# Expert weights that arrive transposed, a program per tile count, and a deferred last down block

## The reference, cut to what matters

```python
slot = jnp.where(kept, experts * C + pos, E * C)
buf = jnp.zeros((E * C + 1, D), x.dtype).at[slot].set(xf[tokens])
xb = buf[:E * C].reshape(E, C, D)
gu = jnp.einsum('ecd,efd->ecf', xb, w12)          # w12: (E, 4096, 512)
g, u = jnp.split(gu, 2, axis=-1)
h = jax.nn.silu(g) * u
yb = jnp.einsum('ecf,edf->ecd', h, w3).reshape(E * C, D)   # w3: (E, 512, 2048)
ys = yb[jnp.minimum(slot, E * C - 1)] * (weights * kept.astype(weights.dtype))[:, None]
out = jnp.zeros((T, D), x.dtype).at[tokens].add(ys)
```

## Time and profile before

| | us |
|---|---|
| median of 3 runs | 3138.96 (3138.65 to 3143.81) |
| profiled execution: span from first to last instruction | 3142.4 |
| first stage, up to the first weight load of the second | 599.4 |
| second stage | 2543.0 |
| TensorE (PE) busy | 3009.2 (96%) |
| VectorE (DVE) busy | 1519.7 (48%) |
| ScalarE (ACT) busy | 1078.7 (34%) |

### The profile page before, as it was taken

How to read it: one execution, slowest core, us unless ns; L and a number is a source line. 1 busy time by engine, 2 the same in 40 slices (tenths; PEclk the granted TensorE clock), 3 DMA queues, 4 the chain that set the end, 5 groups by cost and what they waited for, 6 DMA issues and landing times.

```text
span 3142.4 us, 58679 instructions
## 1 busy us (share of the span) xinstructions
PE 3009.2 (96%) x21454; PEld 2800.7 (89%) x21455; DVE 1519.7 (48%) x3173; ACT 1078.7 (34%) x2999; POOL 412.9 (13%) x393
## 2 busy tenths in 40 slices
PE   6999999599999999999999999999999999999998
PEld 5888888599998999989998999899998999899887
DVE  5777777344444444444444444444444444444444
ACT  5776765122223222232223322322223222332333
POOL 3545554100002000010001000200002000100110
PEclk9999999699999999999999999999999999999999
DMA  7421221311112210230113211220113211321321
GB/s 257 171 86 68 95 74 68 128 55 41 40 40 51 76 40 26 48 92 25 40 40 75 77 41 40 65 76 21 40 41 53 76 40 40 55 91 60 76 89 51
DMA packets 120226, 209.69 MB, mean 67 GB/s; under 512 B 11628, under 2 KB 45180, under 8 KB 119970
## 3 DMA queue, kind: packets, MB, share of 16 engines
q1 hardware_dynamic: 103330, 174.77, 15.8%
q0 software_dynamic: 16640, 31.69, 5.2%
HBM read 145.06 MB, written 67.70 MB: 68 GB/s over the span
## 4 chain that ended last, share of the span: by engine, by line
PE 78%; issue 2%; DVE 1%; ACT 0%; DMA 0%; ACTq 0%; POOL 0%; DVEq 0%; SPq 0%; POOLq 0%
PE bank L1367 71%; PE bank L1382 6%; DVE yacc L1325 0%; DVE w_lo L1288 0%; ACT w_hi L1222 0%; ACT slotsT_hi L1222 0%; DMA raw<-in_L_ffn_w_dram 0%; DVE slotsT_lo L1288 0%; ACT yout L1255 0%; POOL out_dram L1179 0%; DVEq L1058 0%; ACTq L1214 0%; ACTq L1058 0%; DVEq L1035 0%; DVE h_lo L1309 0%
## 5 line engine op out<-in xcount | busy, mean ns | idle before, releaser
L1367 PE MATMUL bank<-slotsT_hi,w_hi 128*128 128x256 f32 x4352 | 1242.2, 285 | 37.5 <-issue 37.5
L1367 PE MATMUL bank<-slotsT_lo,w_hi 128*128 128x256 f32 x4352 | 1223.8, 281 | 0.0
L1367 PE MATMUL bank<-slotsT_hi,w_lo 128*128 128x256 f32 x4352 | 1222.6, 281 | 0.0
L1367 PEld LDWEIGHTS bank<-slotsT_hi,w_hi 128*128 128x128 f32 x4352 | 825.5, 190 | 43.6 <-issue 39.5
L1367 PEld LDWEIGHTS bank<-slotsT_lo,w_hi 128*128 128x128 f32 x4352 | 825.1, 190 | 4.1
L1367 PEld LDWEIGHTS bank<-slotsT_hi,w_lo 128*128 128x128 f32 x4352 | 823.5, 189 | 0.0
L1305 DVE TENSOR_TENSOR h<-silu,bank 128x256 f32<-128x256 f32 x544 | 229.1, 421 | 835.9 <-PE bank L1367 835.9
L1241 ACT CAST h_hi<-h 128x256 fp32r<-128x256 f32 x544 | 221.1, 406 | 814.7 <-DVE h L1305 814.7
L1325 DVE TENSOR_TENSOR yacc<-bank,yacc 128x512 f32<-128x512 f32 x441 | 304.6, 691 | 226.3 <-PE bank L1367 216.1
L1367 PE MATMUL bank<-w_hi,h_hi 128*128 128x512 f32 x1008 | 399.2, 396 | 5.8 <-issue 4.3
L1179 POOL DMA_INDIRECT out_dram<-yout,token x63 | 98.1, 1557 | 2317.2 <-ACT yout L1255 2305.5
(11 more groups left out here) (157 smaller groups left out, 3071.1 us busy)
## 6 DMA issues: line engine op xcount, KB each, us to landing
raw<-in_L_ffn_w_dram SPq DMA_DIRECT2D x195, 512.0 KB, 4.4
xrow<-expert_rows SPq DMA_DIRECT2D x41, 520.0 KB, 8.9
expert_rows<-zeros SPq DMA_DIRECT2D x40, 520.0 KB, 7.6
xin<-in_x_dram SPq DMA_DIRECT2D x16, 512.0 KB, 3.5
xres<-in_x_dram SPq DMA_DIRECT2D x16, 512.0 KB, 3.5
out_dram<-xres SPq DMA_DIRECT2D x16, 512.0 KB, 3.5
probs<-in_L_xattn_Wq_dram SPq DMA_DIRECT2D x1, 1024.0 KB, 8.7
probs<-in_L_xattn_Wo_dram SPq DMA_DIRECT2D x1, 1024.0 KB, 6.2
```

The source lines that it names most:

```text
L1367: last = nc.tensor.matmul(out_ap, st, mv, start=(at == 0), stop=(at == n - 1))
```

## The change

The host lays both weight tensors out anew, as one array with the contraction on the partitions, each chunk's 1.5 MB contiguous by partition. The kernel loads a chunk with one DMA, and ACT and DVE split it straight from SBUF; PE transposes no weights. In place of the branches in each chunk, every engine picks once per expert among eight complete programs, one for each number of tiles from 3 to 10 (`by_tiles`). Each cuts its tiles into blocks of 2, 3 or 4 tiles (256, 384 or 512 slots), without a padded tile. The down products of a chunk's last block are made after the first gate and up block of the next chunk. In the last chunk the next expert's first four token tiles are transposed between the down products (`closing`).

```diff
-            def blocks(eng, n_e, g1, g2, skip, between, half, end):
+            BLOCKS = {3: (3,), 4: (2, 2), 5: (3, 2), 6: (3, 3), 7: (4, 3), 8: (4, 4), 9: (3, 3, 3), 10: (4, 3, 3)}
+            TILES = sorted(BLOCKS)
+            XA = 4
...
+            def units_at(nt, q):
+                plan = {1: ((0, 1), (2, 3)), 2: ((0,), (1, 2), (3, 4), (5,)), 3: ((0,), (1,), (2,), (3,), (4,), (5,))}
+                return plan[len(BLOCKS[nt])][q]
+            def late_units(nt):
+                return (4, 5) if len(BLOCKS[nt]) == 1 else ()
...
+            def by_tiles(eng, n_e, body):
+                def pick(sizes):
+                    if len(sizes) == 1:
+                        body(sizes[0])
+                        return
+                    with eng.If(n_e > sizes[0] * P):
+                        pick(sizes[1:])
+                    with eng.Else():
+                        body(sizes[0])
+                pick(TILES)
...
+                    def load_weights(e, c, par):
+                        sp.dma_start(raw[par][:, :], w_moe[bass.ds(e, 1), c, :, :].rearrange("e p w -> (e p) w"))\
+                          .then_inc(raw_loaded[par], 16)
...
+                            sp.wait_ge(w_lo, units_before(e, c + 1))
                             load_weights(e + (c + 2) // NCH, (c + 2) % NCH, c % 2)
```

PE in one chunk, after the change:

```diff
+                        def g1(b):
+                            W = BLOCKS[nt][b] * P
...
+                            if b == 0:
+                                pe.wait_ge(w_lo, units + NU12)
+                                if first:
+                                    pe.wait_ge(xa_lo, XA * (e + 1))
...
+                                passes(GB[q % 2][:, 0:W], list(zip(stat(j), moving))).then_inc(g_ready, step_of(nt, q))
+                                if first:
+                                    rest_of_slots(q, 0)
...
+                                passes(UB[q % 2][:, 0:W], list(zip(stat(NJ + j), moving))).then_inc(u_ready, step_of(nt, q))
...
+                        for b in range(nb):
+                            g1(b)
+                            if last and b == nb - 1:
+                                break
+                            if b == 0 and not first:
+                                for t in block_tiles(nt, nb - 1):
+                                    g2(t, nb - 1, True)
+                            elif b > 0:
+                                for t in block_tiles(nt, b - 1):
+                                    g2(t, b - 1, False)
+                        if last:
+                            for kind, i, earlier in closing(nt):
+                                if kind == "x":
+                                    if i % 2 == 0:
+                                        pe.wait_ge(xrow_loaded[i // 2], 16 * (e + 2))
+                                    if i >= 2:
+                                        pe.wait_ge(xa_lo, XA * (e + 1) + i - 1)
+                                    turn(i, xa_tp)
+                                else:
+                                    b = next(b for b in range(nb) if i in block_tiles(nt, b))
+                                    g2(i, b, earlier)
```

DVE in one chunk, after the change (`add` waits for PE's down product of a tile and adds it to `yacc`):

```diff
+                            for j in range(NJ):
...
+                                nc.vector.tensor_tensor(h32[q % 2][:, 0:W], silu[q % 2][:, 0:W], UB[q % 2][:, 0:W], ALU.mult)\
+                                  .then_inc(h32_ready, step_of(nt, q))
+                                if j == NJ - 1 and downs:
+                                    add(downs[0], at, opens)
...
+                                nc.vector.tensor_tensor(h_lo[hb][:, j, 0:W], h32[q % 2][:, 0:W],
+                                                        h_hi[hb][:, j, 0:W].bitcast(fp32), ALU.subtract)\
+                                  .then_inc(hlo_ready, step_of(nt, q))
...
+                                units(units_at(nt, q))
+                            for t in downs[1:]:
+                                add(t, at, opens)
```

POOL makes the zero tiles' DMAs first and then those of the tiles with tokens, in order:

```diff
+                        def scatters(nt):
+                            for t in reversed(range(NT)):
+                                if t < nt:
+                                    wait_apart(pool, "pool", yout_ready, NT * (e + 1) + nt - t)
+                                i = nt - 1 - t if t < nt else t
```

More of the change, by code:

```diff
@@ L22, in flamingo_gated_layer @@
     router_w: bass.AP,
-    w12: bass.AP,
-    w3: bass.AP,
+    w_moe: bass.AP,
     out: bass.AP,
@@ L48, in flamingo_gated_layer @@
     SCALE = float(DK) ** -0.5
-    E, F2, _ = w12.shape
-    F = F2 // 2
+    E, NCH, _, WCOLS = w_moe.shape
     TOPK = 2
@@ L1094, in units_between, with whole @@
[L1094 to L1104 removed]
+                    def whole(nt):
+                        chunk(nt, e, 0, 0, 0, True, False)
+                        with eng.Fori(0, NCH // 2 - 1) as pair:
+                            for i in (1, 2):
+                                chunk(nt, e, pair * 2 + i, i % 2, pair + 1, False, False)
+                        chunk(nt, e, NCH - 1, (NCH - 1) % 2, NCH // 2, False, True)
@@ L1265, in between @@
-                        def between():
-                            for kind, i, place in units_between(first, last):
-                                hi_half(kind, i, 1 - par, units + place)
-                        blocks(act, n_e, g1, g2, skip, between, lambda s: None, lambda s, left: None)
-                        for u in range(NU12, NU):
-                            hi_half("U", u, 1 - par, units + place_of("U", u, first, last))
+                            if last and 0 < b < len(BLOCKS[nt]) - 1:
+                                for t in block_tiles(nt, b - 1):
+                                    scaled(t)
@@ new lines, in _, with chunk, units, add @@
+                    for i in range(XA):
+                        x_low(i, xa_hi, i + 1, xa_lo)
+                    def chunk(nt, e, c, par, half, first, last):
+                        base, tiles = steps_before(e, c), tiles_before(e, c)
+                        def units(which):
+                            for i in which:
+                                w_low(1 - par, i, units_before(e, c + 1))
+                        nb = len(BLOCKS[nt])
+                        def add(t, at, opens):
+                            dve.wait_ge(y_ready, at + t + 1)
+                            b_last = t in block_tiles(nt, nb - 1)
+                            if opens:
@@ L1344, in end @@
-                        def end(s, left):
-                            dve.sem_inc(y_ready, BT * left)
-                            dve.wait_ge(y_added, tiles_before(e, c) + BT + BT * s)
-                            dve.sem_inc(y_added, BT * left)
-                        def between():
-                            for kind, i, place in units_between(first, last):
-                                lo_half(kind, i, 1 - par, units + place)
-                        blocks(dve, n_e, g1, g2, skip, between, half, end)
@@ L1355, in chunk @@
-                        for u in range(NU12, NU):
-                            lo_half("U", u, 1 - par, units + place_of("U", u, first, last))
+                                if b_last:
+                                    dve.wait_ge(y_cleared, e + 1)
+                                dve.wait_ge(y_added, at + 2)
+                                nc.vector.tensor_tensor(yacc[:, t, :], YB[t % 2][:, :], yacc[:, t, :], ALU.add)\
+                                  .then_inc(y_added, tile_of(nt, t))
```

523 lines of the change are left out of this document (251 added, 272 removed).

## The result

The changed kernel takes 2901.1 us (median of 4 runs, 2895.2 to 2903.2) against 3141.2 for the kernel before, measured beside it (3138.7 to 3143.8). The ratio is 0.9232, 95% interval 0.9221 to 0.9244. The forecast was 2899 us, so the total was right to 0.1%. The profiled execution has a span of 2901.4 us against 3142.4: -241.0.

A forecast was written before the change was run, and what follows sets the result against it. PE's own work was taken as the bound, busy 96% of the span. Terms summed to -240 us, from 3142.4 to 2902 for the profiled execution, 2899 us timed; 2860 to 2945 was to hold 8 in 10.

The forecast's parts named there:

- weight transposes: On PE, all 1560 weight transposes go, 195 x 0.875 us, all on the path: -171 us.
- blocks: Gate/up products in blocks of 2 to 4 tiles: -124 us, 113 from padded half blocks, 11 from width itself.
- changes of expert: Between experts, eleven new far jumps on PE at 4.2 us, +46, plus seven times 0.5 us for comparisons.
- start: At the kernel's start, split after the whole load, token tiles behind weights, first expert's far jump: +3 us.
- fourth down tile in blocks of four: PE's fourth down tile waits for DVE's second add, 0.2 us in 32 chunks: +6 us.
- closing: At an expert's end, the third token tile waits for DVE about 1.1 us, half counted as new: +4 us.
- small waits that go: Issue idle ahead of down products of the small experts, 4.3 us, goes: -4 us.
- end: At the kernel's end, the zero tile's DMA stands first instead of last: -2 us.
- Hidden jumps: Rival: queued matmuls mostly cover the eleven far jumps, costing 15 us in place of 46; 2868 us, chance 14%.
- chained exits: Rival: each nested If is left by its own jump, about +125 us; 3024 us, chance 7%.
- small waits in chunks: Rival: PE lacks cover at block borders, 0.7 us in each of 160 block steps, +112; 3011 us, chance 11%.
- late weights: Rival: the single weight DMA lands in 20 us in small experts, 45 in large; 3145 us and more, chance 2%.

The follow-up runs named there:

- even_tiles: Changed kernel with programs for 4, 6, 8 and 10 tiles alone, five experts padded by one tile each; 3050.1 us, ratio 0.9714.
- early_x: Changed kernel with up to four of the next expert's token turns moved between the blocks of an expert's last chunk; 2900.4 us, ratio 0.9234.
- hint_early: As direct_hint, but the hint stands at the start of each program instead of before its last chunk; 2812.9 us, ratio 0.8953.
- hint_loop: Changed kernel with a hint at the top of the loop over experts that its closing branch will be taken; 2885.0 us, ratio 0.9185.
- direct_hint: Changed kernel with tile-count tests in a row, each program branching back itself, and a hint for that branch before the last chunk; 2813.3 us, ratio 0.8952.
- one_program: Changed kernel with only the ten-tile program, no If on the tile count, every expert padded to ten tiles; 3407.1 us, ratio 1.0849.
- no_defer: Changed kernel with the last block's down products made at the end of their own chunk; 2918.9 us, ratio 0.9298.

## Why the prediction was right

Term by term, forecast and found, between the two profiled executions:

| term | forecast | found | from |
|---|---|---|---|
| weight transposes | -171 | -168 | 1536 of the 1560; the others are in the start |
| token transposes | -3.5 | -4 | behind the first product 256, before 296 |
| blocks | -124 | -143 | distances below |
| changes of expert | +49.5 | +57 | 94.4 against 37.5 |
| start | +3 | +6.7 | first product 620.51 against 613.77 |
| fourth down tile in blocks of four | +6 | 0 | no gap in any such chunk |
| three tiles | +2 | +3.2 | one `w_lo` wait |
| closing | +4 | +12 | 14.4 against 2.3 |
| small waits that go | -4 | -10.5 | 6.7 issue, 2.3 `w_lo`, 1.5 `h_lo` before, none after |
| end | -2 | +2.4 | PE's last instruction to the span's end, 13.6 against 11.2 |
| in no term | 0 | +3.2 | what is left of the measured sum |
| sum | -240 | -241 | measured -241.0 |

The first three rows are still counts times distances; what PE's work lost by the trace is 312 us, and the row in no term is the difference.

The steps that carried the result were right: what bounds the kernel (PE's work), the price of the transposes, the padding, and the new far jumps, which are paid nearly in full. Idle at a change was named as about 9 us to ten tiles and 13 otherwise; it was 12.0 to 13.4 to ten or nine tiles and 13.5 to 15.7 to the smaller ones. Hidden jumps (14%) are out by the branch rows, chained exits (7%) by one exit record per expert, small waits in chunks (11%) by the pieces of 312 us, and late weights (2%) by the landing of 1536 KB in 6.2 us.

But 0.1% is better than the steps deserve. Terms were mis-sized both ways, and their errors cancelled. The main ones:

- **Width, -19 too little.** The distance of 384-wide products is 0.1735 us, below both ends of the line that I drew (0.1750 to 0.1769), and a 512-wide gate/up product takes 0.2293, where the 0.2333 of the earlier trace rows belongs to a down product. 5760 x 0.0021 + 1536 x 0.0040 = 18 us. The two kinds differ in their operands' tiles; taking one's price for the other was the mistake. The Trainium skill's rule (TensorE: Matmul & The Clock Gate, section "Wait — 56ns, not 53.3ns?") would have 0.1625 and 0.2158 here, an estimate worked out from it; the trace still disagrees, by 11 and 13 ns. The 75 us that the prediction names for it hold the 384-wide products alone; with the 512-wide ones it would have been 102.
- **Ends of an expert, 12 + 2.4 in place of 4 - 2.** In `closing` two waits appear in every expert, one for `slotsT_lo` (mostly 0.84 us) and one for `yacc` (0.89), for I had followed only the third turn. At the end of the kernel the last DMA still starts 3.3 us behind PE's last instruction, as before. The DMA of zeros no longer stands last, but the eight transposes behind the last product went as well, and three DMAs with tokens now stand in series. And the last one lands later, count and us from issue to landing, before and after:
```profile
out_dram<-nothing,token POOLq DMA_INDIRECT x1, 3.1
...
out_dram<-yout,token POOLq DMA_INDIRECT x1, 5.5
```
Together that is 12 us too little in the forecast.
- **Changes of expert, 7.5 too little.** Seven exits took 31.0 us and three entries 12.1, where eleven jumps at 4.2 had been put in, 46: the exits cost somewhat more, and the entry into nine tiles, priced as far, has no long record at the fifth change. The loop's branch, which was left at its 5.0, took 43.9 us in all against 34.5, and those 9 us were not in any term. The lower clock after the idle time cost what it had cost before, about 2 us, though the idle time was more than twice as long.
- **Start, 4 too little.** The first expert's entry takes 6.1 us; in `even_tiles`, which needs no such jump there, the first product comes 9.6 us earlier.

The width's error made the forecast gain too small, the three others made it too large. On the width's side stand two more, 6 us for a wait that never came (the fourth down tile; it exists, but in the expert with two blocks of four, which only `even_tiles` runs) and 6 us more of small waits that went than I had counted. The errors add up to some 30 us each way, and that they cancel to 1 us is luck; the range of 2860 to 2945 was the fairer statement.

## What to carry to other kernels

Price a jump like any other instruction: read the sequencer's branch records, and where a big body is repeated lay the code out so that its end is one branch back, with a hint ahead of it; here that was worth 88 us, three times what the width of the blocks gave beside the padding (some 30). A wait that is taken out in front of a far jump gains nothing as long as the jump is there (`early_x`: 0.8 us with it, 11 without it), so look at what follows on the same queue before a stall is called a gain. When products of a new width have to be priced, take the price of the same operands at each width, and don't carry it from another kind of product.

## What was not expected of the hardware

- With a hint a far branch on PE takes 0.23 us in place of 4.6, and the hint may stand some 300 us and three taken inner branches ahead (`hint_early`); in `hint_loop`, where the branch stands right behind another far jump, it saves less (4.3 in place of 6.1). The Trainium skill (Runtime: NRT & Kernel Launch, section "Instruction fetch mechanics") says that a taken branch outside the fetched window waits for a DMA; the branches of 3.2 us and more without a hint agree, and with a hint the wait is gone.
- Jumps into a program behind the row of tests cost nothing in `direct_hint` where that program is the one of ten or nine tiles (0.24 to 0.70 us of idle time in all), and 4.1 to 4.6 us for the smaller ones that lie farther on. The first expert's, into nine tiles, is an exception: 5.9 to 7.4 us in every kernel that has it.
- The jumps aren't PE's alone. At the second change of the changed kernel VectorE makes no instruction for 4.1 us behind the comparison that leaves the program and for 5.1 behind the loop's branch, ScalarE for 3.8 and 4.9, though their branch records are 0.04 to 0.06 us; on these engines the time stands behind the record, on PE in it.
- In `one_program` PE idles again for 1.4 to 2.8 us right behind the first product of an expert, which no wait for another engine explains; it is part of the 5.6 us.
- An idle time of 0.2 to 1.0 us leaves PE's granted clock at 2.4 GHz, one of 4 us and more is followed by about a dozen products at 1.2 GHz; of the eight of 1.3 to 2.2 us in `no_defer`, five are followed by a stretch at 1.2 GHz.
- ScalarE's copy of 128x512 takes 617 ns from SBUF, where it took 586 from a bank; VectorE's subtraction takes 0.69 us from either.
